# Attention kernel: the second projection of a group moved from the 16th to the 30th score product, side work taken two tiles at a time

## The reference

```python
n_heads = 16
qkv = (layernorm(x) @ Wqkv + bqkv).reshape(B, L, 3, n_heads, 16)
scores = jnp.einsum('bqhd,bkhd->bhqk', q, k) / math.sqrt(16)
scores = scores + slopes[None, :, None, None] * -abs(pos[None, :] - pos[:, None])
probs = jax.nn.softmax(scores, axis=-1)
out = jnp.einsum('bhqk,bkhd->bqhd', probs, v).reshape(B, L, 256)
x = x + out @ Wout + bout
```

## Time and profile before

| what | value |
|---|---|
| median of 3 runs | 3258.13 us (3257.17 to 3265.41) |
| the profiled execution | 3271.27 us, its span 3269.5 us |
| mean granted TensorE clock in it | 0.952 |
| PE busy | 3085.7 us (94%) |
| DVE busy | 2534.6 us (78%) |
| ACT busy | 1985.8 us (61%) |
| POOL busy | 1094.2 us (33%) |
| attention, first to last column product | 1248.7 to 2917.9 us |

### The profile page before, as it was taken

The page is one execution under the profiler, slowest core; times in us unless marked ns, Lnnn a source line. Parts: engine busy times, 40 slices in busy tenths (PEclk is TensorE's granted clock), DMA queues, the critical chain, the costliest instruction groups (busy, mean ns, idle before and its releaser), DMA issues. The chain is left out here.

```text
span 3269.5 us, 73440 instructions
## 1 busy us (share of the span) xinstructions
PE 3085.7 (94%) x28196; PEld 1827.7 (56%) x28196; DVE 2534.6 (78%) x5875; ACT 1985.8 (61%) x2967; POOL 1094.2 (33%) x1364
## 2 busy tenths in 40 slices
PE   7999999995999869999999999999999999988999
PEld 3666666664788734444454444444544445437888
DVE  6677877764788658888888889788888887927887
ACT  2455444441666515777777777767777777775665
POOL 3354554443223221332423333323233232222222
PEclk8899999985999958999999999999999999998999
DMA  1000000002111151324232323232322322202111
GB/s 54 2 28 28 28 28 28 20 10 73 66 59 59 39 108 36 58 39 83 40 67 55 57 63 60 43 77 52 71 48 49 74 49 53 57 18 93 52 60 38
DMA packets 126461, 165.34 MB, mean 51 GB/s; under 512 B 23584, under 2 KB 104240, under 8 KB 125456
## 3 DMA queue, kind: packets, MB, share of 16 engines
q1 hardware_dynamic: 115688, 149.37, 18.7%
q0 software_dynamic: 9984, 10.38, 2.4%
q10 hardware_dynamic: 440, 0.90, 0.1%
HBM read 81.58 MB, written 38.24 MB: 37 GB/s over the span
## 5 line engine op out<-in xcount | busy, mean ns | idle before, releaser
L1855 ACT ACTIVATE b_p_t<-banks 128x1024 f32<-128x1024 f32 x1024 | 1040.2, 1027 | 304.0 <-PE banks L1742 238.7
L1681 PE MATMUL banks<-b_k_stack,b_q_stack 62*128 62x512 f32 x2048 | 809.6, 475 | 26.5 <-issue 10.8
L1742 PE MATMUL banks<-b_q_stack,b_k_stack 64*128 64x512 f32 x2048 | 767.8, 450 | 9.9 <-ACT b_p_t L1855 9.9
L1941 DVE CUSTOM_DVE_ANT_1 banks<-banks,b_near_rows 128x512 f32<-128x512 f32 x960 | 649.0, 715 | 138.3 <-PE banks L1681 135.1
L1944 DVE TENSOR_REDUCE b_half_max<-banks 128x1 f32<-128x512 f32 x1024 | 657.8, 684 | 79.9 <-PE banks L1681 76.3
L1696 PE MATMUL banks<-b_p_t,b_v 128*17 128x256 f32 x8192 | 631.8, 386 | 6.3 <-POOL b_p_t L2100 5.5
L1742 PEld LDWEIGHTS banks<-b_q_stack,b_k_stack 64*128 64x128 f32 x2048 | 313.7, 185 | 389.1 <-issue 325.5
L2100 POOL TENSOR_TENSOR b_p_t<-b_p_t,b_fall 128x256 f32<-128x256 f32 x384 | 280.5, 733 | 658.6 <-ACT b_p_t L1855 657.8
L1681 PEld LDWEIGHTS banks<-b_k_stack,b_q_stack 62*128 62x128 f32 x2048 | 341.9, 188 | 111.6 <-DVE b_half_max L1941 35.9
L1696 PEld LDWEIGHTS banks<-b_p_t,b_v 128*17 128x17 f32 x8192 | 142.8, 95 | 300.7 <-issue 162.2
L1148 ACT ACTIVATE ffn_relu<-banks,ffn_scale_fc 128x512 f32<-128x512 f32 x256 | 176.2, 688 | 205.5 <-PE banks L1080 205.5
(11 more groups left out here) (255 smaller groups left out, 5333.6 us busy)
## 6 DMA issues: line engine op xcount, KB each, us to landing
ffn_x<-x SPq DMA_DIRECT2D x32, 512.0 KB, 3.9
b_q_stack<-b_qk_hi SPq DMA_DIRECT2D x252, 64.0 KB
b_k_stack<-b_qk_hi SPq DMA_DIRECT2D x252, 64.0 KB
b_fall<-c_fall SPq DMA_DIRECT2D x48, 256.0 KB, 2.6
a_x<-hidden_states SPq DMA_DIRECT2D x16, 512.0 KB, 3.9
x<-a_x SPq DMA_DIRECT2D x16, 512.0 KB, 2.9
x<-ffn_x SPq DMA_DIRECT2D x16, 512.0 KB, 2.8
b_x<-x SPq DMA_DIRECT2D x8, 1024.0 KB, 5.6
```

The source lines that it names most:

```text
L1681: pe.matmul(m, q_stack[rows, slot, qb * P:(qb + 1) * P], k_stack[rows, slot, half * BANK:(half + 1) * BANK], start=True, stop=True, tile_p ...
L1742: last = pe.matmul(out, k_stack[stack, slot, kb * P:(kb + 1) * P], q_stack[stack, slot, half * BANK:(half + 1) * BANK], start=True, stop=n ...
L1855: act.activation(p_t[use % P_BUFS][:, :, :], scores[use % 2], ACT.Exp, scale=slopes()[pair][0]).then_inc(p_made, 1)
L1941: dve.tensor_tensor_reduce(out=m, in0=m, in1=near_window(pair, qb, rg), scale=1.0, scalar=LOWEST, op0=ALU.add, op1=ALU.max, accum_out=larg ...
```

## The change

- `attend` yields after two steps and not after one, so side work stands between pair-steps only.
- `STACKS` goes from 2 steps with weight 3 to 12 steps with weight 1, of which the second and the sixth (`STACK_STEPS = {1: 0, 5: 1}`) hold the two projections.
- The high part of queries and keys comes from GpSimd (a CAST of `qk`) and no longer from ScalarE.
- Values, transposed outputs and projected outputs go two tiles at a time, through one whole bank: 4 steps where 8 were.
- The turned maxima are copied by VectorE and no longer by ScalarE, and they are turned after the fourth row product of the next group, not before the third.

```diff
-        STEPS, STACKS, VALUES, NORMALIZE = GROUP * HALVES * QB, 2, QB, 1 + QB
-        LEAD, TURN = 16, 2
+        STEPS, STACKS, VALUES, NORMALIZE = GROUP * HALVES * QB, 12, QB // 2, 1 + QB
+        STACK_STEPS = {1: 0, 5: 1}
+        LEAD, TURN = 16, 4
...
-                side_by_side(*([(STEPS, attend(g, rows), 1)] if g >= 0 else []),
+                side_by_side(*([(STEPS // ROWGROUPS, attend(g, rows), 1)] if g >= 0 else []),
...
-                             *([(STACKS, stacks(g + 2), 3)] if 0 <= g + 2 < ALL else []),
+                             *([(STACKS, stacks(g + 2), 1)] if 0 <= g + 2 < ALL else []),
...
         def tensor(pe):   # make_values
-                for i in range(QB):
-                    m, (used, n) = misc.take(("v", b, i), (v_made, QB * b + i + 1))
+                for two in range(VALUES):
+                    m, (used, n) = misc.take(("v", b, two), (v_made, VALUES * b + two + 1))
                     pe.wait_ge(used, n)
-                    in_three(m[:, 0:DIM], lambda part, kt: x[part][:, kt, i * P:(i + 1) * P], lambda part, kt: w_v[part][:, kt, :], v_ready)
+                    for j in range(2):
+                        tokens = slice((2 * two + j) * P, (2 * two + j + 1) * P)
+                        last = in_three(m[:, j * DIM:(j + 1) * DIM], lambda part, kt: x[part][:, kt, tokens], lambda part, kt: w_v[part][:, kt, :])
+                    last.then_inc(v_ready, 1)
...
         def scalar(act):   # make_stacks
-                    act.activation(qk_hi[:, cols], m, ACT.Identity, bias=b_scaled[:, hg:hg + 1],
-                                   scale=scale_qk[:, 0:1]).then_inc(qk_hi_made, 1)
...
-                        act.activation(shift_full[:, :], m, ACT.Copy, scale=-1.0).then_inc(shift_copied, 1)
...
         def vector(dve):   # find_maxima
+                    if g and turn == TURN:
+                        dve.wait_ge(max_turned, g)
...
+                        dve.tensor_scalar(shift_full[:, :], misc.at["turn", g - 1][0:2 * GROUP * QB, 0:P], -1.0, None, ALU.mult).then_inc(shift_copied, 1)
...
         def gpsimd(pool):   # make_stacks
+                        pool.tensor_copy(qk_hi[:, cols], qk[:, cols]).then_inc(qk_hi_made, 1)
+                        pool.wait_ge(qk_hi_made, use + 1)
+                        pool.tensor_tensor(qk_lo[:, cols], qk[:, cols], qk_hi[:, cols].bitcast(F32), ALU.subtract).then_inc(qk_lo_made, 1)
...
         def sync(sp):   # make_stacks
-                yield
-                yield
+                for _ in range(max(STACK_STEPS)):
+                    yield
                 sp.wait_ge(bias_cast, 16)
                 sp.wait_ge(qk_hi_made, 2 * (g + 1))
                 sp.wait_ge(qk_lo_made, 2 * (g + 1))
```

More of the change, by code:

```diff
@@ L1657, in make_stacks @@
                 pe.wait_ge(x_lo_made, 4 * (b + 1))
-                for half in range(HALVES):
+                for step in range(STACKS):
+                    if step not in STACK_STEPS:
+                        yield
+                        continue
+                    half = STACK_STEPS[step]
                     cols = slice(half * BANK, (half + 1) * BANK)
@@ L1683, in find_maxima @@
                         yield
+                    if g and turn == TURN - 1:
+                        m, (used, n) = misc.take(("turn", g - 1), (shift_copied, g))
+                        pe.wait_ge(used, n)
+                        pe.wait_ge(row_max_made, g)
+                        pe.transpose(m[0:2 * GROUP * QB, 0:P], row_max[:, :, :].rearrange("p a n -> p (a n)"),
+                                     ident[:, :]).then_inc(max_turned, 1)
+                    if g < ALL:
                         yield
@@ L2084, in conclude @@
                     return
[L2085 to L2089 removed]
+                for n in range(TWOS + 1):
+                    if n:
+                        x, tiles = xs[b % X_BUFS][:, 2 * n - 2:2 * n, :], TWOS * b + n
+                        pool.wait_ge(y_made, tiles)
+                        pool.wait_ge(x_biased, 2 * tiles)
+                        pool.tensor_tensor(x, x, y[:, :, :], ALU.add).then_inc(y_added, 1)
                     yield
```

203 lines of the change are left out of this document (97 added, 106 removed).

## The result

| | before | after |
|---|---|---|
| median, lowest to highest | 3257.65 us, 3252.87 to 3265.41 (4 runs) | 3462.67 us, 3454.51 to 3468.24 (4 runs) |
| ratio to before | | 1.0625 (1.0595 to 1.0655) |
| profiled execution, its span | 3271.27 us, 3269.5 us | 3454.51 us, 3452.7 us |
| mean granted TensorE clock in it | 0.952 | 0.923 |
| attention, first to last column product | 1248.7 to 2917.9 us | 1227.3 to 3094.9 us |

The change makes the kernel 6.25% slower, 205 us by the medians; the prediction said 3414 us, 156 more than before. The busy line of the page shows nothing of a cause: TensorE is busy for 3116.1 us (3085.7 before), VectorE for 2525.1 (2534.6) and ScalarE for 1931.5 (1985.8), about the same work in a longer span.

What follows compares the result with a forecast made beforehand. TensorE sets the pace, VectorE close behind, with little copy margin. 19.6 + 3.0 + 0.8 + 1.0 - 8.0 + 4.8 = 21.2 us a sequence, +156 in all, gives 3414 us, range 3320 to 3495.

Steps and rivals of the forecast that it cites:

- The wait: Before pair-step 24's first row product, TensorE stands still for late bias copies: 19.6 us to a sequence, 3.7 to 7.0 a group.
- The margin: Between the third bias copy's landing and the row product needing it: 2.0 us in group 14, 22.7 to a sequence.
- The savings: Cheaper ring banks, copies and side work gain 2.0 us a group where not swallowed: -8.0 to a sequence.
- Outputs by twos: Three output tiles move ahead of the second projection, +3.0 us to a sequence; shared copies and fewer ring turns get cheaper.
- This stays about level: The maxima's way at group end moves along with the row product, 1.9 us to spare; only first groups cost, +1.0 a sequence.
- The clock: After each wait TensorE's clock may dip: 1.2 us a group (0 to 2.4), +4.8 to a sequence.
- The CAST: High part on GpSimd ahead of the subtraction: 1.0 us for a ScalarE pass of 0.78, +0.8 to a sequence.
- That the copies are in time: Rival: the bias copies land before the row product, only savings are left, 3194 us; chance 0.05.
- That savings repay the stall: Rival: all 2.7 to 3.5 us a group are gained and the clock holds, 3328 us; chance 0.08.
- The third: Rival: the clock doesn't recover and late maxima make TensorE stand twice a group, 3528 us; chance 0.07.

Runs made afterwards that it cites:

- early variant: The changed kernel with the second projection before pair-step 7 and not before 15, all else as changed: 3240.18 us, ratio 0.9943.
- fill kernel: The changed kernel with 18 discarded matmuls of 512 columns ahead of each wait for a group's first head: 3426.52 us, ratio 1.0505.

## Why the prediction was right, and where its terms were off

**The wait: right in place, cause and size.** The margin was read as 2.0 us in group 14 and the delay as 9; the changed trace shows the first copy 7.7 us later in the group, the landing at 2.30 us instead of 2.2, and a wait ended by `b_k_bias` in every one of the 30 groups. The third bias copy is issued 15.0, 11.1, 6.4 and 9.3 us later in groups 12 to 15 than before (at 1990.19, 2052.77, 2107.31 and 2163.97), 41.8 together. The prediction's terms make 41.3 (42.3 + 3.0 + 0.8 - 4.8), so the sum is right, though the 7 to 11 us that it named for each group miss two of the four. It had the row product 18.6 us to a sequence later (19.6 + 3.0 + 0.8 less savings of 4.8); it is 19.5. Undoing the place of the projection removes the wait and the loss, and the place alone, in the kernel before, brings both. The total of 151 us on TensorE lies in the 100 to 170 that the prediction named.

**The savings: three to four times too large, beside an early projection.** They were booked at 2.0 us a group, 64 us over 32 groups; with the wait taken out they are 17.9 us, 0.6 a group, or 33.2 without the doubled outputs. Beside a late projection they are 44.0, to which the last paragraph of this section comes back. Two of the steps behind the price were wrong.

- *Outputs by twos* were booked as a saving of ring turns and ScalarE passes. No saving shows: the kernel without them is 15.3 us shorter in its attention. In the timeline of the changed kernel's group 12 the 12 projecting products of two tiles and their four transposes stand in one piece between two pair-steps. From the start of one pair-step to that of the second after it are 5.23 us (1955.75 to 1960.98); less two pair-steps of 1.28 that is 2.67 us for two tiles, 1.3 each, where a single tile was priced at 1.0. Eight tiles would make 2.4 us to a sequence; the first groups themselves differ by 0.7 us. So it is shown that they save nothing; the cause and the size of the 15.3 us are not.

```profile
1955.75 0.50 PE L1757 MATMUL banks<-b_q_stack,b_k_stack 64*128 64x512 f32 x1
...
1958.93 0.39 PE L1629 MATMUL banks<-b_w_out_hi,b_att_hi 128*128 128x256 f32 x1
...
1960.98 0.50 PE L1757 MATMUL banks<-b_q_stack,b_k_stack 64*128 64x512 f32 x1
```

- *The second group of a sequence* was taken to gain like the others and loses: in group 13 56.48 us in the early variant against 53.81. VectorE has the statistics of the layer norm (3.3 us) in one piece early in the group, and empties no ring bank meanwhile. Before, the first projection stood on TensorE (1943.86) beside them (from 1944.04), and what remained of the wait for VectorE was 1.12 us. In the changed kernel this projection comes a pair-step and a half later, and TensorE stops for 2.67 us:

```profile
2011.79 2.71 DVE L1884 BATCH_NORM_STATS2 b_stats<-b_x 128x6 f32<-128x256 f32 x8
...
2015.80 0.50 PE L1685 MATMUL banks<-b_k_stack,b_q_stack 62*128 62x512 f32 x1 [2.67 <-DVE b_half_max L1953]
```

and the same place in the trace of before, the first projection and the row product that waits:

```profile
1943.86 0.50 PE L1627 MATMUL banks<-b_x_hi,b_w_qk_hi 128*128 128x512 f32 x1
...
1948.05 0.50 PE L1681 MATMUL banks<-b_k_stack,b_q_stack 62*128 62x512 f32 x2 [1.12 <-DVE b_half_max L1944]
```

The variant with the first projection one pair-step earlier halves this wait, to 1.3 us at the longest, and its second groups are as short as before the change (53.6 us in the mean, 54.0 before, 55.4 in the early variant).

**"This stays about level": wrong.** The prediction let the maxima's way move along with the row product and charged 1.0 us in first groups only. Behind the row product the four groups got 7.9 us longer, where +4.8 for the clock, +1.0 for the maxima and -3.2 of savings make +2.6. In group 14 the way from row product to load is 3.2 us longer: 1.6 up to the transpose, of which 1.2 is the half clock (the fill kernel has 2.08 where the changed one has 3.28) and 0.4 the later place of the transpose; and 1.6 from there to the load, for the CAST behind a third product with the table. In the fill kernel, at full clock and with the same queue, this last stretch is 6.0 us (2105.84 to 2111.84), 7.0 in the changed kernel and 5.4 before. With 1.9 us to spare, 3.2 us can't be free; in group 14 it shows as 1.7 us more from row product to group end. In the first group (12) it is 3.9 us, with the same sequence of store, load and maxima on SyncE's queue as in the kernel with the other order of heads. Before, store and load of the maxima stood 4.3 us apart in this group (1933.69 and 1937.98); now it is 6.25. That queue was named, its price was too low:

```profile
1995.11 0.39 SPq L2191 DMA_DIRECT2D x<-b_x  x1
1999.64 0.38 SPq L2136 DMA_DIRECT2D b_x<-x  x1
2000.13 0.54 SPq L2166 DMA_DIRECT2D b_shift_dram<-b_shift  x1
2006.38 0.55 SPq L2170 DMA_DIRECT2D b_q_stack<-b_shift_dram  x2
```

**The clock: right for the changed kernel, by the fill.** Booked at 1.2 us a wait, worth 1.2 us a wait. By the Trainium skill (TensorE: Matmul & The Clock Gate, the section on HAM oscillation) each such wait lets TensorE restart at the half clock, and the trace agrees: in group 14 the clock is 0.50 for the 6.6 us after the gap, and each of the 30 waits has half clock beside it. The 6.6 us at half speed alone would be 3.3 us; that less comes out is in part the longer wait for the maxima in the fill kernel, and the rest was not taken apart. The forecast would have come to some 3450 us with the full 2.4 us a wait, nearer to the 3463 measured, but by the fill that price is not the reason for the miss. In the kernel before with the late projection the half clock lasts longer and was not priced by a fill.

**The CAST: below both bounds.** Booked at 1.0 us, between 0.78 and 1.28, it is 0.608, against 1.275 for the subtraction of the same size. In the place of a ScalarE pass of 0.78 us it shortens the way to the copies by 0.2 us a group, where the forecast had it 0.2 longer:

```profile
L2069 POOL TENSOR_TENSOR b_qk_lo<-b_qk,b_qk_hi 128x512 fp32r<-128x512 f32 x64 | 81.6, 1275 | 5.3
...
L2067 POOL CAST b_qk_hi<-b_qk 128x512 fp32r<-128x512 f32 x64 | 38.9, 608 | 338.5 <-ACT b_qk L1810 338.3
```

The GPSIMD Engine Reference of the Trainium skill, section 4.1, puts GpSimd at about twice VectorE's time with two inputs and near line rate with one. The trace has VectorE at 0.738 us for such a subtraction (L1274) and 0.496 for such a CAST (L1272), so GpSimd takes 1.7 and 1.2 times as long. The estimate of 0.64 us that the prediction worked out from it was the better price here.

**The rivals.** That the copies are in time fell with the first row of waits. That savings repay the stall fell with the time itself, and with the early variant, which has 17.9 us of them where that rival wanted 2.7 to 3.5 a group. The third, that a second wait appears at the group's end, is partly true: 11 to 16 times, 10.7 us in all on the matmuls and 18.8 on their weight loads, not in every group. It comes forward where the first wait is shortened (84.9 us with the wanted head first) and where the clock is kept (37.2 us with the fill).

**What the numbers leave open.** Predicted were +21.2 us to a sequence, measured +27.4 in groups 12 to 15 and 195.7 over the attention, 26.1 for each of 7.5 sequences. Which term is to blame for the difference, some 49 us in the time, depends on where one starts. From the early variant, the late place costs 213.6 / 7.5 = 28.5 where 19.6 + 3.0 + 0.8 + 1.0 + 4.8 = 29.2 were booked, and the savings are 2.4 (17.9 / 7.5) where 8.0 were: the costs are right and the savings missing. From the kernel before, the late place costs 239.7 / 7.5 = 32.0 where 19.6 + 1.0 + 4.8 = 25.4 were booked, and all the rest gives back 5.9 (44.0 / 7.5) where 8.0 - 3.0 - 0.8 = 4.2 were: the savings are there, and the late place was priced too low. Its error lies behind the row product, where it costs 15.2 us to a sequence (487.3 - 373.6 over 7.5) and the clock and the maxima had been booked at 5.8. The two parts don't simply add, and the prediction took it that they do. That the rest of the change softens the stall behind the row product is seen there, with a higher clock beside it; the cause was not tested.

## What to carry to other kernels

Before work that feeds a long row of DMA issues is moved, subtract: the time from the last issue that counts, plus its landing, to the instruction that needs it is all the delay that is free, and here it was 2 to 9 us of a group of 50. Then follow the same queue further down, since what stands behind the issues gets late as well: with the first wait shortened, the second came to light and kept some 90 us of the 205. Don't book a gain for fewer and larger pieces of side work where the passes that they save are on engines with time to spare: it was booked here and did not come. And test a part at both ends, taken out of the changed kernel and put into the old one: the late projection cost 214 us the one way and 240 the other.

## What the runs showed of the hardware

- In group 14 of the changed kernel an issue of a 64 KB copy within the core holds SyncE's queue for 0.51 to 0.60 us, and back to back these issues stand 0.55 to 0.65 us apart; 20 of them took 12.37 us (2094.94 to 2107.31). Single issues take longer: one of 1.92 us stands in the same row of the kernel before, which took 13.69 us. The reader of the copy issued last started 2.20 to 2.36 us after its issue.
- A 32 KB store issued right behind a load of a whole sequence came back late: from its issue to the load behind it were 5.1 and 6.3 us with the sequence's load 0.5 us ahead, 4.3 us with it 1.8 us ahead (group 12 of the kernel before), and 1.8 us where no such load preceded.
- The part ahead of the attention, which no kernel here changes, ended at different times in single executions: the load of `b_ident` was issued at 1121.2 to 1140.8 us. Two profiles' spans may differ by 19.6 us for it alone, which is more than several edits here are worth. Even in the attention, the stretch up to the first column product was 102.8 to 110.8 us long; lengths of the groups alone, or ratios of medians over runs, are what can be compared.
- Eighteen discarded matmuls in each wait made the changed kernel 36 us faster; the time at the half clock behind the row products fell from 187 to 23 us.
- GpSimd's CAST of 128x512 took 0.608 us, its subtraction of two such inputs 1.275 us.
